# Layer 0 of a two-layer decoder: one query tile moved ahead of the scores, and decays taken in groups

## The reference, cut to what matters

```python
# L0 attention: 16 query heads, 4 key heads, head size 128, rotary embedding
q = q * cos + rotate_half(q) * sin          # k likewise
qf, kf = elu(q) + 1, elu(k) + 1
# causal linear attention: with state = sum of k v^T up to the position
num, den = qf @ state, qf @ z               # z = sum of kf
out = (num / (den + 1e-6)) @ Wo.T
# L0 xattn: mLSTM, 16 heads of size 32, from x (queries) and the context
log_D = cumulated log forget gates + input gate, -inf above the diagonal
D = exp(log_D - max_log_D)
C = (qh @ kh.T / sqrt(32)) * D
h = C / (max(|C.sum|, exp(-max_log_D)) + 1e-6) @ vh, normalised by head
```

## Time and profile before

| | us |
|---|---|
| median of 3 runs | 2944.35 (2939.48 to 2947.29) |
| the profiled execution | 2941.02, its span 2939.2 |
| TensorE busy in the span | 2685.3 (91%) |
| VectorE busy | 1372.6 (47%) |
| ScalarE busy | 839.4 (29%) |
| GpSimd busy | 588.4 (20%) |
| layer 0 in the span | 0 to about 1100 |

### The profile page before, as it was taken

One profiled execution on the slowest core, in us unless ns is written; L12 is line 12 of the kernel. 1 busy time (PEld: TensorE's weight loads), 2 busy tenths in 40 slices (PEclk: granted clock), 3 DMA queues, 4 the chain that ended last, 5 costly groups with the idle time before them and its releaser, 6 DMA issues. The chain is left out here.

```text
span 2939.2 us, 33813 instructions
## 1 busy us (share of the span) xinstructions
PE 2685.3 (91%) x10989; PEld 1366.4 (46%) x10990; DVE 1372.6 (47%) x2541; ACT 839.4 (29%) x1894; POOL 588.4 (20%) x632
## 2 busy tenths in 40 slices
PE   7998999999999856799999999769599999999998
PEld 3544554554455342344334433153256555666543
DVE  3555554563557263467777777423012222222255
ACT  2324332432343231145545555510001111111101
POOL 2111101110111000322333223004311111111154
PEclk9999999999999878899999999969699999999999
DMA  5120122122102103435545454240113333342144
GB/s 189 58 72 29 58 72 86 58 83 76 57 29 72 43 1 127 76 72 116 101 106 111 108 105 102 61 163 1 35 57 129 129 128 130 105 154 97 63 140 154
DMA packets 110236, 261.00 MB, mean 89 GB/s; under 512 B 21955, under 2 KB 55619, under 8 KB 98211
## 3 DMA queue, kind: packets, MB, share of 16 engines
q1 hardware_dynamic: 95202, 220.27, 25.3%
q0 software_dynamic: 13648, 38.06, 4.4%
q10 hardware_dynamic: 1264, 1.10, 0.1%
HBM read 203.76 MB, written 55.22 MB: 88 GB/s over the span
## 5 line engine op out<-in xcount | busy, mean ns | idle before, releaser
L2395 PE MATMUL d_bank<-d_w,d_xcol 128*128 x1280 | 407.0, 461 | 0.0
L1957 DVE TENSOR_REDUCE c_mx<-c_pair 128x2 f32<-128x1024 f32 x256 | 303.6, 1217 | 110.5 <-PE c_pair L1818 109.5
L1668 ACT ACTIVATE c_probs<-c_exp 128x512 f32<-128x512 f32 x512 | 277.9, 597 | 218.4 <-PE c_exp L1832 215.3
L745 PE MATMUL a_bank<-a_xT,a_ring 128*128 128x512 f32 x640 | 287.3, 600 | 11.2 <-DMA a_ident<-in_ident 11.2
L507 POOL TENSOR_TENSOR a_ry<-a_rt 128x512 f32<-128x512 f32 x80 | 131.4, 1642 | 790.9 <-DVE a_rt L997 790.9
L2395 PEld LDWEIGHTS d_bank<-d_w,d_xcol 128*128 128x128 f32 x1280 | 231.8, 191 | 102.4 <-issue 1.5
L2402 PE MATMUL d_bank<-d_w,d_hid 128*128 (+1 forms) x486 | 221.9, 592 | 0.6 <-DVE d_hid L2596 0.6
L745 PE MATMUL a_bank<-a_wo,a_ot 128*128 128x512 f32 x512 | 222.4, 592 | 0.0
L2336 PE MATMUL d_bank<-d_xT,d_ws 128*128 128x512 f32 (+1 forms) x384 | 179.4, 620 | 34.9 <-issue 34.2
L745 PEld LDWEIGHTS a_bank<-a_xT,a_ring 128*128 128x128 f32 x640 | 120.8, 193 | 150.6 <-issue 137.2
L1832 PE MATMUL c_exp<-c_qs,c_ks 128*128 128x512 bf16 x512 | 160.3, 384 | 16.0 <-ACT c_probs L1668 7.6
(11 more groups left out here) (299 smaller groups left out, 3765.5 us busy)
## 6 DMA issues: line engine op xcount, KB each, us to landing
d_w<-in_w SPq DMA_DIRECT2D x16, 1408.0 KB
scratch_results<-d_yrow SPq DMA_DIRECT2D x81, 256.0 KB
a_ring<-in_wq SPq DMA_DIRECT2D x16, 1024.0 KB, 4.8
a_wo<-in_wo SPq DMA_DIRECT2D x16, 1024.0 KB, 4.8
c_ks<-scratch_kpark SPq DMA_DIRECT2D x96, 128.0 KB, 4.4
c_qs<-scratch_qpark SPq DMA_DIRECT2D x96, 128.0 KB, 4.4
d_w<-in_w SPq DMA_DIRECT2D x16, 768.0 KB
a_ring<-in_w SPq DMA_DIRECT2D x8, 1024.0 KB, 8.4
```

The source lines that it names most:

```text
L745: ins = pe.matmul(bank[:, :], lhs(c), rhs(c), start=(c == 0), stop=(c == n - 1))
L1668: act.activation(probs[:, (LC * CH * n + k) % RING, :], bank[:, :], ACT.Exp, scale=float(CD) ** -0.5).then_inc(exped.sem, 1)
L1957: dve.tensor_reduce(mx[:, n % 2, at0:at0 + 2], bank[:, :].rearrange("p (i n) -> p i n", i=2), AX.X, ALU.max).then_inc(maxed.sem, 1)
L2395: ins = pe.matmul(bank[:, 0:FI], xcol[:, v, k, :], w13[:, bass.ds(at, 1), which, k, :].rearrange("p a n -> p (a n)"), start=(k == 0), stop ...
```

## The change

Two orders change. On TensorE, in the list of banks and on VectorE the first query tile of key head 1 (and its rotary parts) goes ahead of the scores of key head 0 (on VectorE ahead of the mask). On ScalarE the decays of quarters 1 and 3 become one group of four ahead of the second query's exponential; two decays of quarter 2 go ahead of the fourth query's; in quarter 0 the fourth decay goes behind the last query's exponential. No instruction is added or dropped.

```diff
--- before.py
+++ after.py
@@ -306,10 +306,10 @@
             spread_of(m, 0)
             a_tiles(a, "q", *queries_of(0, range(3, 4)))
             scores_of(m, 0)
+            a_tiles(a, "q", *queries_of(1, range(1)))
             a_tiles(a, "s", *of_b(0))
             values_of(a, 0)
 
-            a_tiles(a, "q", *queries_of(1, range(1)))
             spread_of(m, 1, range(2))
             a_tiles(a, "q", *queries_of(1, range(1, 2)))
             spread_of(m, 1, range(2, 4))
@@ -679,29 +679,28 @@
                 values(3)
                 query_elus(0, range(3))
                 floors()
-                decay_of(0)
+                decay_of(0, range(3))
                 query_elus(0, range(3, 4))
+                decay_of(0, range(3, 4))
                 scaled(0)
 
                 query_elus(1, range(1))
-                decay_of(1, range(2))
+                decay_of(1)
                 query_elus(1, range(1, 2))
-                decay_of(1, range(2, 4))
                 turned_out(0)
                 heads(0)
                 query_elus(1, range(2, 3))
                 decay_of(2, range(2))
                 squares(0)
+                decay_of(2, range(2, 4))
                 query_elus(1, range(3, 4))
-                decay_of(2, range(2, 4))
                 heads(1)
 
                 scaled(1)
                 query_elus(2, range(1))
-                decay_of(3, range(2))
+                decay_of(3)
                 squares(1)
                 query_elus(2, range(1, 2))
-                decay_of(3, range(2, 4))
                 turned_out(1)
                 heads(2)
                 query_elus(2, range(2, 3))
@@ -923,10 +922,10 @@
                 spread(0)
                 queries(0, range(3, 4))
                 head_scores(0)
+                queries(1, range(1))
                 scores(0)
                 attended(0)
 
-                queries(1, range(1))
                 spread(1, range(2))
                 queries(1, range(1, 2))
                 spread(1, range(2, 4))
@@ -1246,10 +1245,10 @@
                 if a == 0:
                     dve.wait_ge(late.sem, 16 * NL)
                 weigh_scores(0)
+                query(1, 0)
                 mask(0)
                 sums(0)
 
-                query(1, 0)
                 query(1, 1)
                 weigh_scores(1)
                 query(1, 2)
```

## The result

| | before | after |
|---|---|---|
| median, us | 2939.26 (6 runs, 2938.72 to 2947.29) | 2911.60 (6 runs, 2906.40 to 2918.54) |
| the profiled execution, its span | 2941.02, 2939.2 | 2911.83, 2910.0 |
| ratio, 95% interval | | 0.9889 (0.9876 to 0.9903) |
| layer 1 begins at | 1145.19 | 1118.05 |

The account below looks back on a forecast made before the run. TensorE bounds the kernel, so its standing still counts: 5.1 + 16.7 + 7.4 = 29.2 us won, less 4 for slow clock, gives 25 and 2919 us against the median 2944.35. The range is 2909 to 2932.

Parts of the forecast that it names:

- stage 0: Query tile fills TensorE's 6.08 us wait before key head 0's scores: gain 5.1 us, of which 1.6 is clock.
- scores to second head scores, three stages: Stages 1 to 3, tile moved and quarter 1's decays grouped: gains 4.9, 5.5 and 6.3 us, together 16.7.
- second to fourth head scores, three stages: Key head 2, quarter 3's decays grouped: 3.07 wait goes, about 2.4 comes before head scores; 2.5 us a stage, 7.4 in three.
- stage 4: The stage without queries: ScalarE's order said to be what it was, so 0 us won.
- the rest of layer 0, put down to clock: About half of 8.5 us slow clock behind four long waits taken as given back: 4 us off the gain.
- The moved waits: New TensorE waits: 2.1 us before value products, 1 before second head scores, about 2.4 before key head 2's head scores.
- the fourth decay's delay: Quarter 0: fourth decay behind the last query's exponential ends at 256.4 instead of 254.0, making VectorE's weighing 0.5 us later.
- The weights came in time: Stage 0: the moved tile's weights land by 52.5 at worst, before its start at 55.46; each us later would cost one.
- quarter 2 moved nothing in stages 1 to 3: Two decays moved ahead of an exponential stay covered by the output products: 0 us.
- the grouping was not empty: Rival: ScalarE reaches the second exponential late, key heads 1 and 2 keep their waits; gain 12, time 2933 us; chance 0.11.
- the gain in clock was lost again in part, not entirely: Rival: each new wait is followed by a half-rate stretch; gain 15, time 2929 us; chance 0.13.
- nothing slower: Rival: more, shorter waits keep TensorE at 1.2 GHz through stages 0 to 3; 17 us slower, time 2961; chance 0.03.

Follow-up runs that it names:

- the second pair: Changed kernel and kernel before, both unaltered, run and traced again on one chip: ratio 0.989; layer 1 begins at 1116.49 and 1145.35 us.
- groups alone: ScalarE's decay order of the changed kernel, the query tile left behind the scores, against the kernel before: ratio 0.9938; layer 1 begins at 1129.39 us.
- quarter 0's decays together: Changed kernel with quarter 0's four decays together ahead of the last query's exponential: ratio 0.9863 to the kernel before; layer 1 begins at 1114.66 us.

## Why the prediction was right or wrong

Step by step, in us won, from the first pair of traces:

| step | forecast | measured |
|---|---|---|
| stage 0 | 5.1 | 3.5 (70.19 + 3.43 - 69.80, less 0.3 by which this run's scores began earlier) |
| scores to second head scores, three stages | 16.7 | 15.0 (3.25, 5.50, 6.26) |
| second to fourth head scores, three stages | 7.4 | 8.9 (2.55, 3.51, 2.85) |
| stage 4 | 0 | 2.3 |
| the rest of layer 0, put down to clock | -4 (for all places) | -2.9 (what is left of 26.8) |
| layer 0 | 25 | 26.8 |
| behind layer 0 | 0 | 2.1, in the second pair 0.6 |

**What held.** The bound and the places: the order of waits was read right, from the query tile in the gap to the masks behind the rotary parts. The value products begin 5.59 after the scores (257.89 - 252.30), forecast 5.6. The second head scores follow the scores by 21.02 in stages 2 and 3, forecast 21.0. The moved waits are 1.89, 1.11 and 2.11, forecast 2.1, 1 and 2.4; the fourth decay's delay reached the masks and costs 0.4 where 0.5 was said, shown by its removal. The weights came in time, no bank of the shifted order held anything, quarter 2 moved nothing in stages 1 to 3.

**What failed.** First, "In stage 4, without queries, the ScalarE order is what it was: 0." That is true of quarter 2 only. In quarter 3 the old order had `squares(1)` between the halves, and without queries the squares stay there; the squares wait 3.23 us for VectorE, the second half stands behind them, and TensorE's fourth head scores behind that, 2.2 us. ScalarE in stage 4 of the kernel before, the squares and the second half:

```profile
1062.37 0.63 ACT L643 ACTIVATE a_work<-a_work 128x512 f32<-128x512 f32 x1 [3.23 <-DVE a_work L1142]
1062.90 2.16 ACT L625 ACTIVATE a_dec<-a_bank,a_am 128x128 f32<-128x128 f32 x8
```

I had looked at what the moved decays pass in stages with queries and read off the rest. All five traces with quarter 3 split have 9.90 from the third to the fourth head scores there, the seven with quarter 3 whole 7.63 or 7.64: 2.3 us, where the prediction had 0.

Second, the size of the clock. I took 4 back, one lump for all. Measured it is 1.6 in stage 0 (scores at 5.17, as before), 1.7 in stage 1's value products and 2.9 elsewhere, so 6.2. Against it stand 1.5 more than forecast between the second and fourth head scores. Of these, 0.8 are second head scores at half rate in stage 2 of the kernel before (1.96), and the rest are mostly its slow head values behind the 3.07 wait, which I had put at 0.5 a stage; they took 3.46, 3.63 and 3.75, where full rate gives 2.16. The net of 4.7 is near the forecast by luck, and the second pair of traces, where stage 0 and the value products were fast, shows that single places can't be forecast.

Third, the end of the range. 2909 stands for 35 us won against the median of 2944.35 that was shown. In six runs the kernel before has a median of 2939.26; from there 2909 leaves 30 us, and the ratio's 1.11% is 32.6. The two pairs of traces show 27.1 and 28.9 in layer 0, 29.2 and 29.5 in the whole span. So in layer 0 the two terms above account for what the first pair shows beyond 25. Behind layer 0 lie 2.1 and 0.6, where I had 0; why is not shown. Whether the few us more in the ratio are real stays open, since the intervals of both sets of runs hold 29.

The rivals: the grouping was not empty (groups alone save 15.8), the gain in clock was lost again in part, not entirely, and nothing slower showed in any run. The rule of the Trainium skill, page "TensorE: Matmul & The Clock Gate", Part 1, is that activity releases the half rate and idling brings it back. Taken alone, for waits shorter than before, it gave 29 and came closer in total than my 25. That is luck as well, since 2.3 of the measured sum are stage 4, and the rows do not follow it place by place: the same wait of 2.65 in stage 0 is followed by scores of 5.1 to 5.2 in four of nine traces and of 3.70 in five.

## What to carry to other kernels

Where an engine waits for the last of a chain, put there the next independent tile whose weights and bank are ready; then list who is queued behind each piece it drags along, on every engine, since that is where the next wait stands (here masks behind rotary parts, 1.9 us, gone by weighing in VectorE's idle time before). When a call moves past others that return at once in some stages, go through the order of each kind of stage by itself. Count the slow clock behind a wait as part of the wait's price, and forecast a range for it, not the places.

## What the runs showed of the hardware

Behind the longest waits TensorE always ran slow, behind the shortest never; between them the length of the wait doesn't settle it. The cases of stages 1 to 3 (of stage 0 for 2.65) in all traces, with waits that agree to 0.03 us except where a span is given:

| wait, us | what follows, us | slow |
|---|---|---|
| 3.90 | scores, 5.19 to 6.67 in place of 3.70 | 9 of 9 |
| 3.07 | head values, 3.13 to 3.75 in place of 2.16 | 15 of 15 |
| 2.65 to 2.72 | scores, 5.1 to 5.2 in place of 3.70 | 4 of 9 |
| 2.07 | head values | 0 of 3 |
| 1.89 | value products, 5.45 in place of 3.81 | 3 of 9 |
| 1.76 | head values, 2.95 in place of 2.16 | 1 of 9 |
| 1.46 | value products | 0 of 6 |
| 1.15 | second turning of the normalised rows, 3.43 to 4.32 in place of 2.92 | 20 of 36 |
| 0.28 | scores | 0 of 27 |

The turning is slow more often behind 1.15 than the value products behind 1.89, so something besides the wait counts; what it is, no run here shows. Three waits of 3.9 filled with useless matmuls gave 6.6 us back in one trace, and 1 to 6 in the times.

Chip 6 is 45 to 47 us faster than chips 10 and 7 on the kernel before, and the traces show it in one line of the last part, the shared experts' matmuls. In all four traces of chip 6 they stand idle 0.7 us ahead and are busy 168 to 169, in the eight others they stand idle 35 to 37, nearly all of it for no releaser that the profile shows, and are busy 179 to 182. Here are the changed kernel's first trace and quarter 0's decays together (chip 6), in the view of lines, TensorE, behind layer 0; the numbers behind the bar are busy us, mean ns of one, and idle us with what ended it.

```profile
L2335 PE MATMUL d_bank<-d_xT,d_ws 128*128 128x512 f32 (+1 forms) x384 | 179.6, 620 | 36.0 <-issue 35.3 <-ACT d_yrow L2315 0.7
```

```profile
L2334 PE MATMUL d_bank<-d_xT,d_ws 128*128 128x512 f32 (+1 forms) x384 | 168.6, 599 | 0.7 <-ACT d_yrow L2314 0.7
```

What stops TensorE there is not shown.
